# Linear attention with modulated layer norms: the first modulation applied to the turned x, its columns from one-column products, and the next x turned ahead of the q feature

## The reference, cut to what matters

```python
mod = (silu(c) @ wmod).reshape(1, 6, 1, 512)       # c: 1 x 512, wmod: 512 x 3072
sa, ca, ga, sb, cb, gb = mod[:, 0], ..., mod[:, 5]  # ga, gb: magnitude at least 0.25
h = layernorm(x) * (1 + ca) + sa                    # x: 1 x 8192 x 512
q = elu(h @ Wq.T + bq) + 1                          # 16 heads of 32
k = elu(h @ Wk.T + bk) + 1
v = h @ Wv.T + bv
KV = einsum('bhsd,bhsm->bhmd', k, v)
Z = 1.0 / (einsum('bhsd,bhd->bhs', q, k.sum(axis=2)) + 1e-6)
x = x + ga * (einsum('bhsd,bhmd,bhs->bshm', q, KV, Z) @ Wo.T + bo)
h = layernorm(x) * (1 + cb) + sb
x = x + gb * routed_ffn(h)                          # 8 experts, the two best of each row
```

## Time and profile before

| | us |
|---|---|
| median of three runs | 1182.32 (1181.68 to 1182.43) |
| the profiled execution | 1182.51, span 1180.8 |
| PE busy | 1163.4 |
| DVE busy | 980.5 |
| ACT busy | 539.2 |
| POOL busy | 601.9 |

### The profile page before, as it was taken

How to read it: one execution, slowest core, us unless ns; L and a number is a source line. 1 busy time by engine, 2 the same in 40 slices (tenths; PEclk the granted TensorE clock), 3 DMA queues, 4 the chain that set the end, 5 groups by cost and what they waited for, 6 DMA issues and landing times.

```text
span 1180.8 us, 18181 instructions
## 1 busy us (share of the span) xinstructions
PE 1163.4 (99%) x5456; PEld 969.5 (82%) x5456; DVE 980.5 (83%) x2242; ACT 539.2 (46%) x1095; POOL 601.9 (51%) x458
## 2 busy tenths in 40 slices
PE   8999999999999999999999999999999999999998
PEld 5888888788887788888788888888888888888886
DVE  6998788988889988887788888888888888888875
ACT  4555445455544545555353434434435344354441
POOL 1434443433343443443565666667666666676632
PEclk9999999999999999999999999999999999999999
DMA  6565544543443434444413453444544544445321
GB/s 231 167 194 179 168 138 135 160 135 107 124 128 107 141 110 132 121 141 125 108 46 114 148 164 129 145 153 127 165 137 141 162 132 144 145 138 164 112 86 54
DMA packets 168834, 161.01 MB, mean 136 GB/s; under 512 B 16712, under 2 KB 115440, under 8 KB 168736
## 3 DMA queue, kind: packets, MB, share of 16 engines
q1 hardware_dynamic: 168736, 159.85, 43.7%
HBM read 95.30 MB, written 64.49 MB: 135 GB/s over the span
## 4 chain that ended last, share of the span: by engine, by line
PE 80%; DVE 8%; ACT 4%; issue 4%; POOL 2%; DMA 1%; SPq 0%; DVEq 0%; POOLq 0%; ACTq 0%
PE ps L1727 25%; PE ps L1728 25%; PE ps L1734 25%; PE ps L1948 1%; PE ps L1940 1%; POOL cn L758 1%; DVE zk L1381 1%; ACT exp_k L903 1%; DMA wm_in<-in_L_wmod_dram 1%; DVE qf L1357 1%; PE ps L1835 1%; ACT exp_q L874 1%; ACT exp_q L876 1%; DVE zk L1393 1%; ACT exp_k L905 1%
## 5 line engine op out<-in xcount | busy, mean ns | idle before, releaser
L730 POOL TENSOR_TENSOR xn_lo<-xn,xn_hi 128x512 fp32r<-128x512 f32 x64 | 86.1, 1345 | 275.0 <-ACT xn_hi L865 275.0
L746 POOL TENSOR_TENSOR qks<-q_in,ks_q 128x1024 f32<-128x1024 f32 x32 | 77.0, 2407 | 103.0 <-DVE ws L1566 85.6
L758 POOL TENSOR_TENSOR cn<-c,half 128x16 f32<-128x16 f32 x32 | 93.7, 2927 | 37.7 <-DVE c L1484 37.7
L927 ACT CAST xT_hi<-ps 128x512 fp32r<-128x512 f32 x64 | 37.0, 578 | 153.4 <-DVE ps L1457 145.6
L1727 PE MATMUL ps<-wk_hi,xT_hi 128*128 128x512 f32 x256 | 100.8, 394 | 4.7 <-ACT xT_hi L859 4.7
L874 ACT ACTIVATE exp_q<-qf 128x512 f32<-128x512 f32 x64 | 40.5, 633 | 142.1 <-DVE qf L1357 142.0
L1727 PE MATMUL ps<-k_hi,xn_hi 128*128 128x512 f32 x256 | 101.7, 397 | 0.0
L1727 PE MATMUL ps<-wq_hi,xT_hi 128*128 128x512 f32 x256 | 101.1, 395 | 0.1
L1727 PE MATMUL ps<-g_hi,qT_hi 128*128 128x512 f32 x256 | 100.3, 392 | 0.1
L1727 PE MATMUL ps<-v_hi,xT_hi 128*128 128x512 f32 x256 | 100.0, 391 | 0.0
L1728 PE MATMUL ps<-wk_lo,xT_hi 128*128 128x512 f32 x256 | 99.7, 390 | 0.0
(11 more groups left out here) (251 smaller groups left out, 3239.3 us busy)
## 6 DMA issues: line engine op xcount, KB each, us to landing
xin<-_attn_hidden_states_dram SPq DMA_DIRECT2D x64, 256.0 KB, 3.2
q_scratch<-qf SPq DMA_DIRECT2D x64, 256.0 KB, 3.3
xin<-_attn_hidden_states_dram SPq DMA_DIRECT2D x32, 512.0 KB, 4.5
q_in<-q_scratch SPq DMA_DIRECT2D x128, 128.0 KB, 3.0
out_dram<-qf SPq DMA_DIRECT2D x64, 256.0 KB, 2.2
xn_scratch<-xn SPq DMA_DIRECT2D x62, 256.0 KB, 2.0
xq<-xn_scratch SPq DMA_DIRECT2D x248, 64.0 KB, 2.5
x_scratch<-xn SPq DMA_DIRECT2D x56, 256.0 KB, 2.3
```

Of the source, the lines that this page charges most:

```text
L730: nc.gpsimd.tensor_tensor(moved(xn_lo[:, 1 - s, :], i + 1), kept(xn[:, 1 - s, :], i + 1), moved(f32(xn_hi[:, 1 - s, :]), i + 1), ALU.subtr ...
L746: nc.gpsimd.tensor_tensor(qks[:].rearrange("p h (g f) -> p (h g) f", f=P), q_of(j).rearrange("p (n f) -> p n f", f=P), ks_q[:].unsqueeze(1 ...
L758: nc.gpsimd.tensor_tensor(cn[:].rearrange("p h e -> p (h e)"), c2[:].rearrange("p h e -> p (h e)"), half[:], ALU.pow).then_inc(cn_done, 1)
L927: nc.scalar.copy(xT_hi[:, h, :], bank_x2T).then_inc(x2Th_done, 1)
```

## The change

- The columns: 32 products of a 128 x 128 block of `wmod` as the weight with silu(c) as a single moving column give `sa` and `ca` directly as columns in one PSUM bank. DVE copies them to `mod_col`. The rows, their transposes and the second copies of them are gone; for later uses on other partitions (`mod_col4`) the columns go through DRAM (`mod_scratch`): one store in step 2 and eight loads of single elements in step 4.
- The modulation: it is applied to the turned x in `bank_xT`, in four blocks, before it is rounded: by DVE for tile 0, by ACT for every other tile. The k and q weights are split straight from PSUM without a factor, and the products of `sa` with the weights are gone.
- The start: weights of q and k are loaded in halves behind `wmod`; tiles 1 and 2 are normalised before the columns are there; the first k and q products are interleaved with the turning of the weights.
- The steps: on DVE, `turned_x(i + 1)` stands before `modulation` and `q_feature(i - 1)`; on ACT `xT_high` stands before the exponentials of k.

The diff, cut:

```diff
@@ sync: the loads of the start @@
-            sp.dma_start(raw_k[:], Wk.rearrange("(r p) f -> p r f", p=P)).then_inc(wk_in, 16)
+            def x_load(i):
+                wait_count(sp, xn_done, i - 1)
+                sp.dma_start(xin[:, i % 2, :], xt[rows(i), :]).then_inc(x_in[i % 2], 16)
+
             for b in range(KB):
                 sp.dma_start(wm_in[:, :, b, :], wm[:, b, 0:2, :]).then_inc(wma_in[b], 16)
-            sp.dma_start(raw_q[:], Wq.rearrange("(r p) f -> p r f", p=P)).then_inc(wq_in, 16)
-            sp.dma_start(xin[:, 1, :], xt[rows(1), :]).then_inc(x_in[1], 16)
+                if b == 1:
+                    x_load(1)
+            x_load(2)
+            for raw, src, signal in ((raw_k, Wk, wk_in), (raw_q, Wq, wq_in)):
+                for h in range(2):
+                    cols = slice(2 * h * P, 2 * (h + 1) * P)
+                    sp.dma_start(raw[:, :, cols], src.rearrange("(r p) f -> p r f", p=P)[:, :, cols]).then_inc(signal[h], 16)
...
+                if i == 4:
+                    sp.wait_ge(mod_out, 16)
+                    for b in range(KB):
+                        for n in range(2):
+                            sp.dma_start(mod_col4[quarter(b), n, :],
+                                         mod_dram.rearrange("(j d) m -> d m j", d=DH)[:, n * KB + b, :],
+                                         allow_slow_non_contiguous=True).then_inc(mod4_in, 16)
...
@@ scalar @@
+            def modulated(i):
+                act.wait_ge(xTb_done, i + 2)
+                for b in range(KB):
+                    blk = slice(b * P, (b + 1) * P)
+                    nc.scalar.activation(bank_xT[:, blk], bank_xT[:, blk], ACT.Identity, bias=sa1_col[:, b:b + 1],
+                                         scale=ca1_col[:, b:b + 1]).then_inc(xTm_done, 1)
...
             def step(i, s):
                 if i == 0:
                     xT_high(i, s)
                 if live(i - 1, T) and i < T - 1:
                     q_exponential(i - 1, 1 - s)
+                if live(i + 1, T) and i > 0:
+                    xT_high(i, s)
                 prepare(i, 0)
...
-                    if live(i + 1, T) and i > 0:
-                        xT_high(i, s)
                     act.wait_ge(kf_done, i + 1)
...
@@ vector @@
+            dve.wait_ge(mod_psum, 1)
+            nc.vector.tensor_copy(sa1_col, ps[:, MOD_BANK, 0:KB]).then_inc(mod_col_done, 1)
+            nc.vector.tensor_scalar(ca1_col, ps[:, MOD_BANK, KB:2 * KB], 1.0, None, ALU.add).then_inc(mod_col_done, 1)
...
@@ vector, step(i, s) @@
-                ahead = live(i + 2, T)
+                ahead = live(i + 2, T) and not early_turn
                 if ahead:
                     statistics(i + 2, s)
                     mean_var(i + 2, s)
                     var_eps(i + 2, s)
+                if live(i + 1, T) and i > 0:
+                    turned_x(i + 1, 1 - s)
                 if 1 <= i <= 4 * KB:
                     modulation((i - 1) // KB, (i - 1) % KB)
...
                 if ahead:
                     normed(i + 2, s)
                 if live(i + 1, T) and not early_turn:
-                    turned_x(i + 1, 1 - s)
+                    xT_low(i + 1, 1 - s)
...
-                if i in (2, 4):
-                    mod_columns(1 if i == 2 else 0)
@@ tensor @@
             turn_x(0, 0)
-            pe.wait_ge(wk_in, 16)
-            for b in range(KB):
-                turn_weight(raw_k, b, K_BANK, k_psum_turned)
             pe.wait_ge(silu_done, 1)
             for b in range(KB):
                 pe.wait_ge(wma_in[b], 16)
-                last = nc.tensor.matmul(ps[:, 0, :], c_col[:, 2, b:b + 1].to_broadcast([P, P]), wm_in[:, 0, b, :],
-                                        start=(b == 0), stop=(b == KB - 1))
+                for n in range(2):
+                    for f in range(KB):
+                        last = nc.tensor.matmul(ps[:, MOD_BANK, n * KB + f:n * KB + f + 1], wm_in[:, n, b, f * P:(f + 1) * P],
+                                                c_col[:, 2, b:b + 1], ...)
...
-            bias_rows("bk", k_turn)
```

More of the change, by code:

```diff
@@ L640, in step @@
                     loads(i)
-            sweep_tiles(step, -2, T - 1)
+            sweep_tiles(step, -1, T - 1)
             q_store(T - 2, 0)
@@ L1155, in _ @@
             normed(0, 0)
+            statistics(1, 1)
+            mean_var(1, 1)
+            var_eps(1, 1)
+            normed(1, 1)
+            statistics(2, 0)
+            mean_var(2, 0)
+            var_eps(2, 0)
+            normed(2, 0)
             def low(j, src, col, hi, lo):
@@ L1174, in _ @@
-            dve.wait_ge(sa_psum, 1)
-            for n in (0, 1):
-                if n == 1:
-                    dve.wait_ge(bias_turned, KB)
-                    taken_by(nc.vector.tensor_copy(small[:, 0:1], mod_turn[:, 0, 0:1]), "sa")
-                    full("sa")
-                for i in range(KB):
-                    last = nc.vector.transpose(groups(mod_turn[quarter(i), n, :]),
-                                               natural(ps[quarter(i), n, :])[:, :, i, :])
-                    last.then_inc(bias_turned, 1)
-                if n == 1:
-                    dve.wait_ge(bias_turned, 2 * KB)
-                    nc.vector.tensor_scalar(ca1_col[:], groups(mod_turn[:, 1, :])[:, :, 0], 1.0, None,
-                                            ALU.add).then_inc(ca_done, 1)
@@ L1188, in _, with weight_low @@
-            for b in range(KB):
-                low(f"k{b}", k_turn[b], ca1_col[:, b:b + 1], wk_hi[:, b, :], wk_lo[:, b, :]).then_inc(wlo_done, 1)
-            statistics(1, 1)
-            mean_var(1, 1)
-            var_eps(1, 1)
-            dve.wait_ge(bias_in, 32)
-            full("bk")
-            taken_by(nc.vector.tensor_tensor(bk_row[:], bank("bk"), bk_row[:], ALU.add), "bk")
-            normed(1, 1)
-            def low_q(b):
-                low(f"q{b}", q_turn[b], ca1_col[:, b:b + 1], wq_hi[:, b, :], wq_lo[:, b, :]).then_inc(wlo_done, 1)
+            def weight_low(j, banks, b, hi, lo):
+                dve.wait_ge(prep_hi, HI[j] + 1)
+                nc.vector.tensor_tensor(lo, ps[:, banks[b], :], f32(hi), ALU.subtract).then_inc(wlo_done, 1)
@@ L1382, in step @@
                 if early_turn:
-                    for b in range(KB):
+                    for b in range(1, KB):
                         low_q(b)
@@ L1395, in step @@
                     scaled(i)
-                    if live(i + 1, T) and not early_turn:
-                        xT_low(i + 1, 1 - s)
                     dve.wait_ge(kf_done, i + 1)
@@ new lines, in first_product @@
+            def first_product(dst, w_hi, w_lo, n, between):
+                x_hi, x_lo = xT_hi[:, 0, :], xT_lo[:, 0, :]
+                for b in range(KB):
+                    blk = slice(b * P, (b + 1) * P)
+                    pe.wait_ge(prep_hi, n + b + 1)
+                    nc.tensor.matmul(dst, x_hi[:, blk], w_hi[:, b, :], start=(b == 0), stop=False)
+                between(0)
+                pe.wait_ge(xTl_done, 1)
+                for b in range(KB):
+                    nc.tensor.matmul(dst, x_lo[:, b * P:(b + 1) * P], w_hi[:, b, :], start=False, stop=False)
+                between(1)
+                for b in range(KB):
+                    pe.wait_ge(wlo_done, n + b + 1)
+                    last = nc.tensor.matmul(dst, x_hi[:, b * P:(b + 1) * P], w_lo[:, b, :], start=False, stop=(b == KB - 1))
+                return last
```

167 lines of the change are left out of this document (76 added, 91 removed).

## The result

The changed kernel takes 1248.96 us (median of 4 runs, 1246.27 to 1250.05) against 1182.25 of the kernel before on the same chip: a ratio of 1.0562, 95% interval 1.0543 to 1.0580. The prediction said slower, 1206, and at most 1226. The direction holds; the size is nearly three times what I forecast (67 for 24).

What follows compares the result with a forecast made beforehand. PE bounds the kernel before; after the change the one-step DRAM round-trip loop does from step 2. 12 us late by step 17, the earlier start included, plus 12 in steps 17 to 62, on 1182.5, gives 1206; range 1186 to 1226.

Steps and rivals of the forecast that it cites:

- The start: Before the k product of tile 1: PE's unbroken stream starts 5.6 us earlier, bounds 0 and 8.
- my 25.5: Start: the k product of tile 1 begins at 25.5 us in place of 31.07.
- Steps 2 to 16: First sweep: the DRAM round trip sets the time, loop 9.5; 12 us late here, the start's gain already inside.
- Steps 17 to 62: Rest of the first sweep: loops and DVE-heavy steps add 12 us against 389.3, from -4 to +22.
- The 8.4: Steps 17 to 62: length of one round-trip loop in us; 45 of them are 378.
- The "9": Steps 17 to 62: us added by weight preparation between zk and the tile on DVE, some 16 instructions in seven steps.
- The "8": Steps 19 to 22: a `cat` job makes DVE's own list the longer, about 2 us each, 8 in all.
- The second sweep: Second sweep: untouched by the change, still 628 us.
- Rival 2: First sweep: full contention, every trip as measured, later stretch at its upper end; 1224; chance 0.13.
- Rivals 1, 3 and 4: First sweep: no contention, 1189, 0.22; round trip not holding DVE, 1172, 0.08; start and loop cancel, about 1182, 0.05.
- rival 1: First sweep: no contention, every trip 6.3, since DVE's wait moves stores clear of loads; about 1189; chance 0.22.

Runs made afterwards that it cites:

- no_trip: Changed kernel with xq loaded as raw, not normalised x from the input at the head of SP's step, without waiting for the store: 1205.85 us.
- wide64: Changed kernel with each column product moving 64 equal columns in place of one, the other 63 not read: 1244.28 us.
- order_only: Kernel before with only the order of the steps on DVE and ACT changed; old start, modulation folded in the weights, no ACT pieces: 1226.66 us.
- order_only_no_trip: Kernel before in the new order, modulation folded, with xq loaded as not normalised x from the input at the head of the step: 1183.14 us.
- order_back: Changed kernel with the DVE and ACT lists of the steps put back in the old order; new start and four ACT pieces stay: 1227.17 us.

## Why the prediction was too low

**The start** (5.6 earlier) was wrong by 5.0, by the clock: the 64 instructions were priced at 0.115 from the earlier trace rows, which PE had done at full clock in the midst of 512-column products. At the start the row's price held for 16 of them, and then the clock halved (in no_trip about 1 us later). wide64, with the clock held, gives my 25.5 to 0.1. The rule that I cited beside it (the Trainium skill, "TensorE: Matmul & The Clock Gate", section "LDWEIGHTS (loading the stationary operand)": 107 ns for 128 columns) fits wide64's 113 ns. The measured 211 are at the other clock level; the trace of before has that level near 655 only, on products with 328 columns, and so no price for a one-column product there.

**Steps 2 to 16** were right, in the mechanism and in the size. The forecast loop was 9.5, a trip of 6.9 with 2.6 of DVE; measured 9.31, 6.90 and 2.41. DVE waits for `xq` in each of the 15 steps. Step 17 is 14.4 late (12 forecast); in wide64, where the start is as forecast, 11.4 (163.60 to 174.96). order_only and no_trip confirm the cause: in the new order the trip alone makes it, and without it the stretch is PE's. My argument about the stores held, and further than I took it: the reload's issue follows the store's by about 2.04 in most steps, where 5.4 had been seen. What makes single trips long is the time from the reload's issue to the transpose, 4.01 on the mean where I had 3.7. The Trainium skill, "DMA: Bandwidth & Descriptors", section "Anatomy of one DMA", states its fixed 2.0 us and the bytes over 436 GB/s for transfers that GpSimd issues; the transfers here are issued by SP. Applied to the store all the same it would have 2.6, and the rows say less. The estimate of the trip that I made from it, 6.6, is close to the 6.90.

**Steps 17 to 62** are the step that failed, +12 forecast and +47.4 measured. In the terms of my sum, 45 loops of 8.4 with 9 and 8 for the jobs of DVE made 395; measured, the 45 loops from the transpose at 175.09 to the one at 610.52 take 435.4:
- The 8.4 was right: 16 loops that end on the DMA and have no job between `zk` and the tile are 8.31 on the mean, none under 8.05.
- The "9", for jobs between `zk` and the tile, measures 18: six loops of 9.6 to 12.4 in place of 8.4.
- The "8" is the term that failed, and measures 41. I let DVE's own list be the longer in four steps. It is so in 22, of 9.2 to 13.8 us, all with a job in the list, and in them DVE does not wait for the DMA at all. (One loop of 7.75 is left.) The kernel had it in print: the table `PREP` gives 21 of its steps a job behind the tile, and I had taken only the four `cat` ones.

The runs show two causes behind these lists:
- The trip. Measured, order_only is 27.8 over the earlier trace rows and order_only_no_trip 1.0, so the trip costs 26.8 without any piece. Before, a step with a long list (9.51 in step 20) borrowed from the room of more than a step in the round trip, and light steps paid it back (7.05 in step 23, against PE's 8.16). With the trip inside one step a light step is nearly always 8.05 or more: nothing is paid back, and the sum goes over the maximum of list and loop in each step. I added means.
- The pieces. I put ACT's chain into the slack of `k_lo` (my 1.15 for four is 1.48) and counted it only in four steps, 8 us. Without the trip it costs 22.0 (412.24 for 390.28); with one piece of 0.75 only 1.7 are left. What they lengthen is not PE's wait for one tile but DVE's list. Here is DVE in steps 20 and 21 of the changed kernel, from one `xT_lo` to the next:
```profile
217.40 0.69 DVE L1134 TENSOR_TENSOR xT_lo<-ps,xT_hi 128x512 fp32r<-128x512 f32 x1 [0.55 <-ACT xT_hi L875]
218.59 0.69 DVE L1393 SCALAR_TENSOR_TENSOR zk<-zk,exp_k 128x512 f32<-128x512 f32 x1 [0.50 <-ACT exp_k L917]
220.03 0.69 DVE L1399 TENSOR_TENSOR k_lo<-zk,k_hi 128x512 fp32r<-128x512 f32 x1 [0.74 <-ACT k_hi L921]
...
225.01 0.73 DVE L1128 STREAM_TRANSPOSE ps<-xq 128x512 f32<-128x512 f32 x1
...
227.90 0.69 DVE L1134 TENSOR_TENSOR xT_lo<-ps,xT_hi 128x512 fp32r<-128x512 f32 x1 [0.55 <-ACT xT_hi L875]
```
From `xT_lo` to `xT_lo` 10.50 us, with 1.8 of waits for ACT in it and the transpose not waiting for the DMA at all. Without the trip the list of step 21, transpose to transpose, is 10.49 with four pieces and 9.79 with one.

In this stretch and in the new order the two nearly add up: 26.8 and 22.0, with 1.0 for the order alone, make 49.8, and 47.4 were measured.

**The second sweep** took 2.0 more, not nothing. order_only, with the old start and no pieces, has the same (629.94), and no_trip, with both new, 0.2 (628.12), so neither the new start nor the pieces explain it.

**The rivals.** Rival 2 was nearest (1224), for the wrong reason: it laid the excess on contention at the DMA queues, and the stores are clear of it. Rivals 1, 3 and 4 all assumed the loop to be short or not binding; order_only excludes them, though rival 1 was right that DVE's wait moves the stores clear of the loads. None held that the pieces are a cause of their own. That they are is shown by order_back, where DVE never waits for the trip and the pieces cost 44.7. My own first theory after the result had missed it too. The range could not hold the time because its upper end, too, had DVE's list as the longer in only a few steps, and took the lists without the waits between two engines that take them in order.

So of the 67 us: the order, by way of the trip through DRAM, costs 44 on the kernel before (order_only), and what came with the pieces, the new start in it, another 22 on top of it. Taken the other way round the pieces come first with 45 and the order adds 22. The 5 us that the start could have given went to the slow clock either way.

What stays open: why the reload takes long in single trips although the store goes at once and clear of loads (from its issue to the transpose 5.13 for tile 10 and 5.29 for tile 17, trips of 7.74 and 7.87), and where the second sweep's 2.0 come from.

## What to carry to other kernels

Where two engines hand a tile to and fro within a step, write down the cycle with both engines' in-order lists and its length beside the bound engine's step; an instruction on an engine that is half idle costs in full, in each step, once that cycle is longer. A transfer's room of more than a step is what lets light steps pay for heavy ones: with it gone, add up the maximum of each step, not the mean. And a TensorE price taken from a few instructions among wide ones did not hold for a run of 64: look at the granted clock of the stretch that the price comes from, and ask whether the new place will have it.

## What the runs showed of the hardware that I had not expected

- TensorE's clock fell from 2.4 to 1.2 GHz with the engine busy (4.53 and then 5.00 of 5.00 us): 0.93 in 5 to 10 us, 0.50 in 10 to 20, after 16 one-column products at 0.115 us, which then took 0.211. With 64 columns each it stayed at 1.00 and an instruction took 0.113.
- In order_back it fell to 0.5 for about 3.4 us five times, each time shortly after one wait of 1.8 to 2.9 us.
- ScalarE's scale and shift within PSUM took 1.48 us for four pieces of 128x128 in a row, 0.37 each, and 0.75 for 128x512 at once: the same elements for half the time.
